# Transposing attention probabilities with small VectorE operations in place of TensorE transposes

## The reference, cut to what matters

```python
s = einsum('bhgnd,bhmd->bhgnm', q, k) * scale + bias
p = softmax(s, axis=-1)
o = einsum('bhgnm,bhmd->bhgnd', p, v)
x = layernorm(x + o.reshape(B, N, 4096) @ wo.T)
```

## Time and profile before

| | us |
|---|---|
| median of 3 runs | 2420.19 (2417.53 to 2421.94) |
| profiled execution, its own time | 2417.93 |
| its span, first to last instruction | 2416.1 |
| TensorE busy | 2332.2 (97%) |
| VectorE busy | 1149.3 (48%) |
| ScalarE busy | 779.5 (32%) |
| GpSimd busy | 753.2 (31%) |

### The profile page before, as it was taken

How to read it: one execution, slowest core, us unless ns; L and a number is a source line. 1 busy time by engine, 2 the same in 40 slices (tenths; PEclk the granted TensorE clock), 3 DMA queues, 4 the chain that set the end, 5 groups by cost and what they waited for, 6 DMA issues and landing times.

```text
span 2416.1 us, 34601 instructions
## 1 busy us (share of the span) xinstructions
PE 2332.2 (97%) x12594; PEld 1878.0 (78%) x12594; DVE 1149.3 (48%) x1956; ACT 779.5 (32%) x1475; POOL 753.2 (31%) x709
## 2 busy tenths in 40 slices
PE   8999999997999989998999999999899999999999
PEld 6888888875555557886788888887788888888877
DVE  3444434447677633434444444445345444544456
ACT  2222222223677731222322222322132233223321
POOL 4122122202343335444222222211443333333233
PEclk9999999998999999999999999999899999999989
DMA  3111111000000123211111111110111011101000
GB/s 142 44 40 35 39 43 43 26 28 9 18 14 16 64 70 122 104 52 54 45 45 28 36 39 44 36 32 1 58 44 36 23 35 39 39 17 35 27 32 36
DMA packets 51427, 102.09 MB, mean 42 GB/s; under 512 B 8593, under 2 KB 11153, under 8 KB 50833
## 3 DMA queue, kind: packets, MB, share of 16 engines
q1 hardware_dynamic: 51344, 100.97, 12.8%
HBM read 98.85 MB, written 2.10 MB: 42 GB/s over the span
## 4 chain that ended last, share of the span: by engine, by line
PE 86%; issue 6%; DVE 3%; POOL 3%; ACT 1%; DMA 1%; SPq 0%; POOLq 0%; DVEq 0%; ACTq 0%
PE banks L261 20%; PE banks L263 19%; PE banks L262 19%; PE banks L532 7%; PE banks L585 4%; PE banks L1171 2%; PE banks L1155 2%; PE banks L544 2%; PE banks L572 2%; PE banks L1137 1%; POOL f_wl L1582 1%; PE banks L1144 1%; PE banks L1107 1%; PE banks L1123 1%; POOL f_il L1590 1%
## 5 line engine op out<-in xcount | busy, mean ns | idle before, releaser
L261 PE MATMUL banks<-xTh,wh 128*128 128x512 f32 x1024 | 421.4, 412 | 9.0 <-DVE xTl L1858 7.4
L263 PE MATMUL banks<-xTh,wl 128*128 128x512 f32 x1024 | 405.6, 396 | 0.0
L262 PE MATMUL banks<-xTl,wh 128*128 128x512 f32 x1024 | 404.1, 395 | 0.0
L261 PE MATMUL banks<-woh,oth 128*128 128x512 f32 x768 | 317.9, 414 | 1.0 <-DVE X L848 0.7
L848 DVE TENSOR_TENSOR X<-banks,X 128x512 f32<-128x512 f32 x192 | 132.6, 691 | 381.1 <-PE banks L263 381.1
L262 PE MATMUL banks<-wol,oth 128*128 128x512 f32 x768 | 306.1, 399 | 0.0
L263 PE MATMUL banks<-woh,otl 128*128 128x512 f32 x768 | 305.0, 397 | 0.0
L929 POOL TENSOR_TENSOR sc_sb<-sc_sb,rs 128x512 f32<-128x512 f32 x96 | 100.0, 1046 | 654.0 <-DVE rs L815 654.0
L672 ACT ACTIVATE q_sb<-banks 128x512 f32<-128x512 f32 x192 | 114.5, 596 | 420.4 <-PE banks L263 420.4
L261 PEld LDWEIGHTS banks<-xTh,wh 128*128 128x128 f32 x1024 | 195.8, 191 | 49.4 <-issue 9.2
L263 PEld LDWEIGHTS banks<-xTh,wl 128*128 128x128 f32 x1024 | 194.9, 190 | 44.9
(11 more groups left out here) (209 smaller groups left out, 4041.6 us busy)
## 6 DMA issues: line engine op xcount, KB each, us to landing
raw<-in_a_in SPq DMA_DIRECT2D x144, 256.0 KB, 2.7
raw<-in_a_out SPq DMA_DIRECT2D x96, 256.0 KB, 2.6
f_q<-in_f_q SPq DMA_DIRECT2D x21, 512.0 KB, 4.2
f_s<-in_f_s SPq DMA_DIRECT2D x21, 512.0 KB, 5.2
X<-in_x SPq DMA_DIRECT2D x1, 2048.0 KB, 10.5
x_craw<-in_ctx SPq DMA_DIRECT2D x8, 256.0 KB, 2.6
x_ct<-in_ctxT_pair SPq DMA_DIRECT2D x16, 128.0 KB, 2.0
f_c<-in_ctxT SPq DMA_DIRECT2D x2, 1024.0 KB, 5.2
```

The source lines that it names most:

```text
L261: nc.tensor.matmul(out, w_hi, x_hi, start=start, stop=False)
L262: nc.tensor.matmul(out, w_hi, x_lo, start=False, stop=False)
L263: return nc.tensor.matmul(out, w_lo, x_hi, start=False, stop=stop)
```

## The change

The probabilities are no longer transposed by TensorE. VectorE transposes them in SBUF, in 16 operations per pair, each over 32 partitions and 128 elements (four blocks of 32x32), into a new buffer `pt` with two slots. A new event `TR` stands for it. ScalarE's copy and VectorE's subtraction of `PT` now read `pt` instead of the PSUM bank. The columns of `pt` come in another order, so the moving operand of `probs_v` is read through a pattern of runs of 32 elements. The event lists are rearranged. `PT0-` now comes right after `U_0` (after `VT1-` in the lists without RMS) instead of after `U_1`, followed by `TR2-`. `TR3-` follows `PT1-`. `TR0` and `TR1` of the current head stand near the end of the iteration. In the tail `PV0-` comes first.

```diff
     if rms:
-        ev = events("U_0 U_1 PT0- WS0- WS1- U_2 PV0- PT1- WS2- WS3- U_3 WO0- PV1- U_4 KT0 PT2- WO1- U_5 KT1 PV2- WO2- SQ0 "
-                    "U_6 PT3- U_7 WO3- SQ1 PV3- SC0 WO4- SC1 U_8 U_9 WO5- SQ2 U_10 U_11 WO6- SQ3 SC2 WO7- SC3")
+        ev = events("U_0 PT0- TR2- U_1 WS0- WS1- U_2 PV0- PT1- TR3- WS2- WS3- U_3 WO0- PV1- U_4 KT0 PT2- WO1- U_5 KT1 PV2- WO2- SQ0 "
+                    "U_6 PT3- U_7 WO3- SQ1 PV3- SC0 WO4- SC1 U_8 U_9 WO5- SQ2 TR0 U_10 U_11 TR1 WO6- SQ3 SC2 WO7- SC3")
     else:
-        ev = events("U_0 VT1- U_1 PT0- WS0- WS1- U_2 PV0- PT1- WS2- WS3- U_3 WO0- PV1- U_4 PT2- WO1- U_5 PV2- WO2- SC0 "
-                    "PT3- WO3- SC1 U_6 PV3- WO4- U_7 WO5- U_8 WO6- U_9 WO7- SC2 U_10 SC3 U_11 VT0")
+        ev = events("U_0 VT1- PT0- TR2- U_1 WS0- WS1- U_2 PV0- PT1- TR3- WS2- WS3- U_3 WO0- PV1- U_4 PT2- WO1- U_5 PV2- WO2- SC0 "
+                    "PT3- WO3- SC1 U_6 PV3- WO4- U_7 WO5- U_8 TR0 WO6- U_9 TR1 WO7- SC2 U_10 SC3 U_11 VT0")
     if not project:
-        return events("WO6-- " + ("" if rms else "VT1- ") + "PT0- WO7-- WS0- WS1- PV0- PT1- WS2- WS3- PV1- PT2- WO0- WO1- "
+        return events("PT0- TR2- PV0- WO6-- " + ("" if rms else "VT1- ") + "PT1- TR3- WO7-- WS0- WS1- PV1- WS2- WS3- WO0- PT2- WO1- "
                       "PV2- WO2- PT3- WO3- PV3- WO4- WO5- WO6- WO7-")
...
+            pt = sb("pt", [P, 2, 512])
...
-            def transpose_probs(i, pair):
-                st.need(pe, "p_ready", 4 * i + pair + 1)
-                st.need(pe, "pt_ready", 4 * i + pair)
-                rows = sc_sb[:, pair, :, :].rearrange("p c s -> p (c s)")
-                for t in range(2):
-                    for c in range(2):
-                        last = nc.tensor.transpose(pb[4][:, (2 * t + c) * P:(2 * t + c + 1) * P],
-                                                   rows[:, (2 * c + t) * P:(2 * c + t + 1) * P], ident[:, :])
-                last.then_inc(A["t_done"], 1)
...
+                by_query = [p[:, :].rearrange("p (a c t i) -> p t c a i", a=4, c=2, t=2) for p in (pth, ptl)]
...
-                            last = nc.tensor.matmul(PVB[b][:, cols], v_part[r, 2 * pair + t, :], p_part[r, cols],
+                            last = nc.tensor.matmul(PVB[b][:, cols], v_part[r, 2 * pair + t, :], by_query[p_part][r, t],
...
+                        st.need(act, "pv_done", 4 * j + n)
-                        nc.scalar.activation(pth[:, :], pb[4][:, :], ACT.Copy).then_inc(A["pt_hi"], 1)
+                        nc.scalar.activation(pth[:, :], pt[:, n % 2, :], ACT.Copy).then_inc(A["pt_hi"], 1)
...
+            def transpose_probs(i, pair):
+                st.need(dve, "pt_ready", 4 * i + pair - 1)
+                st.need(dve, "p_ready", 4 * i + pair + 1)
+                rows = sc_sb[:, pair, :, :].rearrange("p c s -> p (c s)").rearrange("p (ct bk i) -> p bk ct i", bk=4, i=32)
+                for bk in range(4):
+                    for q in range(4):
+                        last = nc.vector.transpose(
+                            pt[32 * bk:32 * bk + 32, pair % 2, q * P:(q + 1) * P].rearrange("p (ct i) -> p ct i", i=32),
+                            rows[32 * q:32 * q + 32, bk])
+                last.then_inc(A["t_done"], 1)
...
-                        nc.vector.tensor_tensor(ptl[:, :], pb[4][:, :], f32(pth[:, :]),
+                        nc.vector.tensor_tensor(ptl[:, :], pt[:, n % 2, :], f32(pth[:, :]),
```

More of the change, by code:

```diff
@@ L579, in probs_v @@
                 st.need(pe, "o_ready", 8 * i + 2 * pair)
+                by_query = [p[:, :].rearrange("p (a c t i) -> p t c a i", a=4, c=2, t=2) for p in (pth, ptl)]
                 for t in range(2):
                     cols = slice(t * G * S, (t + 1) * G * S)
-                    for v_part, p_part in ((vh, pth), (vh, ptl), (vl, pth)):
+                    for v_part, p_part in ((vh, 0), (vh, 1), (vl, 0)):
                         for b in range(2):
                             r = slice(64 * b, 64 * b + 64)
-                            last = nc.tensor.matmul(PVB[b][:, cols], v_part[r, 2 * pair + t, :], p_part[r, cols],
-                                                    start=v_part is vh and p_part is pth, stop=v_part is vl)
+                            last = nc.tensor.matmul(PVB[b][:, cols], v_part[r, 2 * pair + t, :], by_query[p_part][r, t],
+                                                    start=v_part is vh and p_part == 0, stop=v_part is vl)
                 last.then_inc(A["pv_done"], 1)
@@ L615, in run @@
                         transpose_v(j, n)
-                    elif kind == "PT":
-                        transpose_probs(j, n)
                     elif kind == "PV":
@@ L833, in run @@
                         sums(j, n)
+                    elif kind == "TR":
+                        transpose_probs(j, n)
                     elif kind == "PT":
                         st.need(dve, "pt_hi", 4 * j + n + 1)
-                        nc.vector.tensor_tensor(ptl[:, :], pb[4][:, :], f32(pth[:, :]),
+                        nc.vector.tensor_tensor(ptl[:, :], pt[:, n % 2, :], f32(pth[:, :]),
                                                 ALU.subtract).then_inc(A["pt_ready"], 1)
```

## The result

The changed kernel takes 2626.7 us (median of 4 runs, 2623.27 to 2630.66) against 2419.08 us before: a ratio of 1.0856, 95% interval 1.084 to 1.0871. It is slower, as forecast. The prediction was 2573 (2475 to 2635), so the result lies 54 us above it, inside the stated range and 2 us above the forecast's own (2530 to 2625). The profiled execution took 2623.27 us, its span is 2621.5.

The account below looks back on a forecast made before the run. The prediction took PE's own work as the bound, with DVE half idle. Its terms 45 + 71 + 19 + 18 = 153 us on the profiled 2417.93 gave 2571, or 2573 as a median of runs, range 2475 to 2635.

Parts of the forecast that it names:

- the price of TR: On DVE, 16 transposes per pair at 0.30 us from start to start: 4.8 us, with ends of 3.3 and 5.6.
- the wait for `wol`: At WO0, a new wait of PE for DVE's wol, about 5 us in each of 21 iterations.
- the one for `vst`: In xattn1, a new wait of a kv unit on PE for DVE's vst copy, near 4 us.
- The first rival: On DVE, the 32-partition operations overlap, TR = 3.3 us, and no clock is lost: 2485 us; chance 30%.
- What PE saves: Transposes taken off PE: 1.68 us per attending iteration, 40 us in all if PE stayed the bound.
- Iterations without RMS: In attn0 and attn1, WO0 4.0 us later, 0.84 given back: +3.2 us, x 14 = 45 us.
- half a clock loss: Behind each new PE stall the clock may fall: half of 1.7 us, 0.85 x 21 = 18 us; ends 0 and 36.
- Iterations of xattn1: In xattn1, WO0 ends 10.6 us later; with the other terms together +10.2 us, x 7 = 71 us.
- Ends of the stages: In the three tails, WO0 ends later behind DVE's queue: some 6.6 us each, 19 us.
- Head 0: TR0 and TR1 cost nothing, given DVE's idle 4.75 us before the additions of WO6 and WO7; head 0 not treated separately.
- The third: Not slower: TR2 and TR3 fit DVE's idle time, needing TR about 1.2 us: 2405 to 2420 us; chance 5%.
- second rival: Stalls also bring POOL's contention or full clock loss; with TR = 5.6 and 36 us of clock, 2630 us; chance 8%.

Follow-up runs that it names:

- experiment 1: Changed kernel with TR3 moved from in front of WS2 and WS3 to behind WO1, in attn0 and attn1 only; 2530.78 us (1.0472 of before).
- experiment 6: Changed kernel with all transposes still on VectorE, but in halves of 8 placed where VectorE was idle before; 2451.56 us (1.0118 of before).
- experiment 9: VectorE transposes only in steady iterations of attn0 and attn1, placed as in experiment 6; TensorE transposes elsewhere as before; 2402.85 us against 2419.34 (0.9935).
- experiment 4: Changed kernel with 16 transposes per pair, each writing to the partition quarter it reads, ordered by quarter (probabilities misplaced); 2539.13 us (1.0505 of before).
- experiment 3: Changed kernel with the 16 transposes of a pair replaced by 4 over all 128 partitions (probabilities misplaced); 2423.52 us (1.0026 of before).
- experiment 8: Experiment 6 plus four unread TensorE transposes wherever the kernel before transposed probabilities; 2476.34 us (1.0224 of before).
- experiment 2: Changed kernel with 18 unread matmuls on TensorE just before its wait for WS2, in iterations without RMS; 2604.61 us (1.0768 of before).

## Why the prediction was right

**The bound and the direction.** Right. PE had next to no slack at WO0: WS3 was ready at 1330.27 and read by the tenth matmul, which started 2.04 us behind the first, at 1330.93; the prediction said none. VectorE's queue put 10 us of transposes in front of WS2 and WS3, and PE waits 4.83 us there. Of the signs the price of TR, the wait for `wol` and the one for `vst` came as written. The periods did not: attn1's is 75.0 us, not 72 to 74, and xattn1's is 12.5 longer, not 10 to 12. PE's busy time rose by 28 us: its matmuls are shown longer at a lower clock, 0.942 in the mean instead of 0.971. Experiments 1, 6 and 9 show that the place decides and not the sum of work.

**The price of TR.** 0.30 us from start to start was forecast, 0.315 measured (5.04 us for 16; median duration 0.303). The reading of the earlier trace rows, that an operation on other partitions starts only when the one before has ended, holds for 32 partitions as well: experiment 4 changes little else and gets 0.21 in the mean, 0.27 where the partition changes. The first rival (TR = 3.3, 2485 us) falls with it; experiment 4 is close to its case and takes 2539, so the price that the walk gave that case was too low as well. The Trainium skill's rule in "VectorE: DVE Perf Modes", "Two Vector instructions with no wait between them", agrees with both kernels: all 15 steps inside a TR held, and 3 of 15. The same page's 311 ns, in "The three transpose paths", is for a 128x128 transpose of bf16; in float32 one over 128 partitions took 270 ns (experiment 3) and one over 32 took 303. The pattern of runs of 32 in PV's moving operand costs nothing: its matmuls start 0.12 us apart in pairs in both kernels.

**What PE saves.** 1.68 us per attending iteration forecast, 1.5 measured where PE waited for nothing (attn0 and attn1 in experiment 3), 1.2 to 1.9 by experiments 8 and 9. Right.

**Iterations without RMS.** +3.2 and half a clock loss (0.85) forecast, +5.8 measured. Three sizes were off. The clock loss is 1.3 to 1.9 us in every one of them, 1.6 in the mean (experiment 2), where I took half of the 1.7 of the earlier trace rows. The two TRs of 5.04 instead of 4.8 and the short gaps between VectorE's operations put the end of WS3 0.7 us later than the walk. And the walk let WO0 end 0.7 us behind WS3, its addition starting 0.2 later; at full clock the addition starts 1.15 behind WS3 (experiment 2), because six matmuls stand behind WS2, so 0.25 was missing. 3.2 + 1.6 + 0.7 + 0.25 = 5.75, against 5.7 in attn0.

In attn1, where it is 5.9, PT0's `ptl` takes 1.13 to 1.31 us from the second attending iteration on, instead of 0.69. It now reads two operands from SBUF, and GpSimd's multiplication of another pair runs all the while:

```profile
1392.91 2.49 POOL L934 TENSOR_TENSOR sc_sb<-sc_sb,rs 128x512 f32<-128x512 f32 x2
```

In attn0 GpSimd has finished by then and `ptl` takes 0.68. The cost of such an overlap I had seen in WS2 and WS3, but not moved to PT0. I read that from the timeline; no run took GpSimd away. It delays WO0 by 0.6 us in attn1, of which only 0.2 is left in the period.

**Iterations of xattn1.** +10.2 and 0.85 forecast, +12.5 measured. The walk can be laid over the timeline, with U_0's first copy at 1933.57 there and at 2070.23 here:

```profile
2073.33 5.04 DVE L815 STREAM_TRANSPOSE pt<-sc_sb 32x128 f32<-32x128 f32 x16
2078.40 0.42 DVE L746 COPY kst<-banks 128x256 f32<-128x256 f32 x1
...
2080.66 1.29 DVE L856 TENSOR_TENSOR wol<-raw,woh 128x512 fp32r<-128x512 f32 x2 [1.30 <-ACT woh L709]
...
2084.08 1.29 DVE L847 TENSOR_TENSOR otl<-banks,oth 128x512 fp32r<-128x512 f32 x2 [1.01 <-ACT oth L702]
...
2086.09 5.04 DVE L815 STREAM_TRANSPOSE pt<-sc_sb 32x128 f32<-32x128 f32 x16
2091.17 1.29 DVE L856 TENSOR_TENSOR wol<-raw,woh 128x512 fp32r<-128x512 f32 x2
...
2094.88 0.69 DVE L853 TENSOR_TENSOR X<-banks,X 128x512 f32<-128x512 f32 x1 [1.29 <-PE banks L264]
```

It put the end of TR2 at 1941.3 (here, less 136.66: 1941.7), the end of WS3 at 1954.9 (1955.8) and that of WO0 at 1955.6 (about 1958). The mechanism was right in each step; the last step lacks the slow clock. Over the six iterations the mean granted clock is 0.93 where it was 0.97.

**Ends of the stages.** 6.6 each forecast, 9.9, 6.2 and 9.4 measured. Nearly all of it lies ahead of the tail's WO0, as the walk had it: from there to the last WO the tails take 23.6, 23.7 and 25.6 us, before 23.4, 24.1 and 24.1.

**Head 0.** This step failed: of TR0 and TR1 the prediction says "nothing", on the idle times before the additions of WO6 and WO7. In head 0 there are no such additions: PE has only U_9 between U_8 and SC2, without WO6 and WO7, and SC3 waits for VectorE to take the scores of SC2, which it does behind 10.1 us of transposes. The first two lines are attn0, the third is attn1:

```profile
43.79 10.12 DVE L815 STREAM_TRANSPOSE pt<-sc_sb 32x128 f32<-32x128 f32 x32 [0.37 <-POOL sc_sb L934]
54.85 1.97 PE L533 MATMUL banks<-k_sb,q_sb 128*128 128x64 f32 x16 [3.38 <-DVE sc_sb L792]
1231.25 3.64 PE L533 MATMUL banks<-k_sb,q_sb 128*128 128x64 f32 x16 [4.80 <-DVE sc_sb L792]
```

Behind each the granted clock is 0.50 for 3 us in attn0 and 6 us in attn1. Where TensorE transposes pairs 0 and 1 of head 0 (experiment 9), neither wait is there and the growth is 1.5 and 0.1 us. The 1.5 is not the change's: from 28 to 37 us, where the kernels still do the same work, the mean granted clock is 0.62 in that run and in the changed kernel, 0.81 before and in experiment 3. Nothing in the runs says why. So of the 6.9 and 5.4 us by which the first stretches grew beyond a stalled iteration some 1.7, nine us at 0.19 less clock, come from elsewhere; the rest is the two waits and the slow clock behind them. I walked the loop's body and not the copy of it that is written out ahead of the loop.

**The sum.** 45 + 71 + 19 + 18 = 153 forecast; 82 + 87 + 25 + 11 = 205 measured, the clock inside the first two. Of the 52 us missing in the profiled execution, 25 are the iterations without RMS (14 x 1.8: clock 0.7, TR and gaps 0.7, WO0's end 0.25, the rest attn1's `ptl`), 10 those of xattn1, 11 head 0 and 6 the ends. All four have the same sign. The direction and the places were worked out; that the sum stayed inside the range is owed to the range's width, which took in most of the second rival.

**The rivals.** The second one, more contention and the full clock loss, was put at 2630 with 8%: the time is nearly its number, though TR was 5.04 and not 5.6. Of its parts the full clock loss came true where it was measured apart (experiment 2), and GpSimd's contention in one operation of attn1's iterations. The third was tried directly: with TR at 0.88 us the kernel takes 2423.5, against 2405 to 2420 worked out for 1.2; the slower clock in xattn1 was not in that sum.

## What to carry to other kernels

An engine that is half idle on average can still have a place without any slack: before moving work onto it, walk its queue through one iteration of each kind, including the first, which has other neighbours, and look for the result that the bounding engine takes the moment it is ready. The same work behind that place instead of in front of it cost 96 us less here, and moved only where it was hidden it gave 0.65%. A stall costs more than its length where the engine's clock falls behind it.

## What was unexpected of the hardware

- A VectorE transpose of 32 partitions x 128 float32 elements takes 0.315 us from start to start when its input or output starts on another 32 partitions than that of the operation before, and 0.21 in the mean when not (experiment 4). One over all 128 partitions takes no longer (0.27, 0.88 us for four), so the sixteen small ones cost 5.7 times as much as the four wide ones.
- The shown duration changes with it (0.303 against 0.260 us), not only the distance.
- A VectorE subtraction of two SBUF operands of 512 float32 elements took 1.13 to 1.31 us in six iterations of attn1 with a two-operand GpSimd operation running beside it, and 0.68 in attn0 with GpSimd idle.
- A stall of 4.83 us of PE was followed by 6 us at a granted clock of 0.74 and 0.69; with 4.1 us of it filled with matmuls that nobody reads the clock stayed at 1.00.
- Behind groups of one-column matmuls (line 544) and the 64-column ones that follow, the clock fell to 0.50 in some iterations of xattn1 and not in others, with PE busy throughout and the same instructions. Which of them it hits moves an iteration by up to 5 us, and no run settled what decides it.
